# Last stage of a two-layer MoE kernel: fewer clears between gathers, z recomputed instead of stored, the next sequence turned ahead of two whole experts

## The reference, cut to what matters

```
x = x + L0_ffn(L0_cond(x, ...))          # attention, then top-1 of 8 experts
x = x + L1_ffn(L1_cond(x, cond, ...))    # this second line is what the change is about
```

```
gp = leaky(x @ w_gate[e]);  up = x @ w_up[e];  y_e = (gp * up) @ w_down[e]
y  = sum over the token's two experts of topk_w * y_e
z  = y + leaky(x @ sw_gate) * (x @ sw_up) @ sw_down
```

```
pooled = z.mean(axis=1);  logits = pooled @ gate_w.T + gate_b
masked = where(logits < second largest, -inf, logits);  gates = softmax(masked)
out    = sum over e of gates[e] * gelu(z @ expert_w[e].T + expert_b[e])
```

## Time and profile before

| what | us |
|---|---|
| median of 3 runs | 590.78 |
| the runs | 590.07, 590.78, 592.22 |
| span of the profiled execution | 585.8 |
| PE busy | 558.2 (95%) |
| DVE busy | 319.7 (55%) |
| ACT busy | 242.6 (41%) |
| POOL busy | 232.9 (40%) |

### The profile page before, as it was taken

One profiled execution on the slowest core, in us unless ns is written; L12 is line 12 of the kernel. 1 busy time (PEld: TensorE's weight loads), 2 busy tenths in 40 slices (PEclk: granted clock), 3 DMA queues, 4 the chain that ended last, 5 costly groups with the idle time before them and its releaser, 6 DMA issues.

```text
span 585.8 us, 11495 instructions
## 1 busy us (share of the span) xinstructions
PE 558.2 (95%) x3816; PEld 462.9 (79%) x3816; DVE 319.7 (55%) x967; ACT 242.6 (41%) x670; POOL 232.9 (40%) x319
## 2 busy tenths in 40 slices
PE   7999999988999999999999999999999999999895
PEld 4788887744999999988788978888888887776674
DVE  3877757676332225743537754444444444666564
ACT  1555444660211111115544245555555455443342
POOL 2312211042111121007545375555555078777860
PEclk9999999999999999999999999999999999999999
DMA  5960000185995522513396035555555324555562
GB/s 144 390 289 4 1 1 2 63 368 243 333 328 199 184 85 73 155 64 74 72 296 210 0 82 158 157 159 161 161 161 148 99 81 126 170 173 184 158 190 75
DMA packets 51158, 88.16 MB, mean 150 GB/s; under 512 B 9202, under 2 KB 41843, under 8 KB 49556
## 3 DMA queue, kind: packets, MB, share of 16 engines
q1 hardware_dynamic: 42980, 65.16, 31.6%
q0 software_dynamic: 8112, 22.16, 15.7%
HBM read 62.25 MB, written 25.04 MB: 149 GB/s over the span
## 4 chain that ended last, share of the span: by engine, by line
PE 74%; POOL 8%; DVE 7%; issue 4%; DMA 4%; ACT 2%; SPq 1%; POOLq 0%; ACTq 0%; DVEq 0%
PE psum L1326 10%; PE psum L1339 9%; PE psum L1498 9%; PE psum L1586 9%; POOL arena L924 6%; PE psum L1600 5%; PE psum L1182 5%; PE psum L1154 5%; PE psum L1515 4%; PE psum L1578 3%; DMA arena<-x,row_tok 2%; PE psum L1162 2%; PE psum L1661 1%; PE psum L1533 1%; POOL iota_i L954 1%
## 5 line engine op out<-in xcount | busy, mean ns | idle before, releaser
L924 POOL DMA_INDIRECT arena<-x,row_tok x71 | 68.3, 963 | 53.4 <-PE psum L1578 43.4
L924 POOL DMA_INDIRECT arena<-y_sorted,pos_k_i x64 | 64.4, 1006 | 34.7 <-issue 16.2
L1586 PE MATMUL psum<-big_w,arena 128*128 x284 | 73.0, 379 | 0.0
L1916 ACT ACTIVATE arena<-psum,arena 128x128 f32<-128x128 f32 x64 | 18.3, 368 | 106.4 <-PE psum L1326 84.7
L1661 PE MATMUL psum<-big_w,arena 128*128 x248 | 61.3, 379 | 0.0
L1326 PEld LDWEIGHTS psum<-arena,big_w 128*128 128x128 f32 x512 | 59.5, 192 | 1.7 <-issue 1.0
L1326 PE MATMUL psum<-arena,big_w 128*128 128x128 f32 x512 | 59.8, 275 | 0.8 <-DVE arena L2613 0.8
L1498 PE MATMUL psum<-arena,big_w 128*128 128x256 f32 x256 | 59.8, 381 | 0.2 <-ACT arena L1935 0.2
L1586 PEld LDWEIGHTS psum<-big_w,arena 128*128 128x128 f32 x284 | 53.7, 190 | 7.3
L1339 PE MATMUL psum<-arena 128*128 128x256 f32 (+1 forms) x256 | 57.7, 379 | 0.0
L2849 DVE SCALAR_TENSOR_TENSOR arena<-arena 128x128 f32<-128x128 f32 x71 | 20.8, 293 | 60.4 <-ACT arena L2002 57.2
(11 more groups left out here) (338 smaller groups left out, 996.3 us busy)
## 6 DMA issues: line engine op xcount, KB each, us to landing
y_sorted<-arena SPq DMA_DIRECT2D x71, 128.0 KB
big_w<-w SPq DMA_DIRECT2D x8, 1024.0 KB, 5.2
tokens<-x SPq DMA_DIRECT2D x4, 1024.0 KB, 13.2
x<-tokens SPq DMA_DIRECT2D x16, 256.0 KB, 2.6
z_kept<-arena SPq DMA_DIRECT2D x16, 256.0 KB
out<-arena SPq DMA_DIRECT2D x15, 256.0 KB
y_late<-arena SPq DMA_DIRECT2D x16, 128.0 KB, 1.7
big_w<-expert_w_t SPq DMA_DIRECT2D x1, 2048.0 KB, 8.0
```

Of the source, the lines that this page charges most:

```text
L924: pool.indirect_dma_start(dst, None, rows, bass.IndirectOffsetOnAxis(ap=idx, axis=0)).then_inc(done, 16)
L1586: mm = pe.matmul(bank[2 + i % RT][:, 0:2 * M1], c_gt[i % RT][:, k, :], mgu_s[:, k, bass.ds(e, 1), :].rearrange("p a m -> p (a m)"), start= ...
```

## The change

- POOL calls `space()` only after the gathers of the first three sequences (b < RT).
- SP no longer stores `z_t`, and ACT no longer waits for that. In the case of ties POOL gathers the rows of each sequence again (`rows_again`, with the indices copied to `pos_b`), DVE sums them, PE turns and ACT copies them. This adds a branch at the end of POOL's program that waits for `d_all`.
- PE's step c now turns sequence c + 1 first, then loads the indices of c, does the whole first expert of c, the logits of c + 1, and the whole second expert of c.
- DVE's step b now has `sum_choices` of b + 1 ahead of `gates` of b.

```diff
@@ POOL
                 for n, k, done in parts:
                     gather_rows(yk[b % RT][:, 2 * n + k, :], y2_dram, pos_k_i[:, b * NB + n, k:k + 1], done)
-                    space()
+                    if b < RT:
+                        space()
+            with pool.If(more_gates(pool)):
+                with pool.Fori(0, B) as b:
+                    rows_again(b)
@@ SP
-            for b in range(B + 2):
-                if 2 <= b <= B:
-                    sp.wait_ge(d_res, b - 1)
-                    sp.dma_start(outr[:, (b - 2) * NB:(b - 1) * NB, :], res[(b - 2) % RT]).then_inc(d_st[(b - 2) % RT], 16)
-                if b < B:
-                    sp.wait_ge(d_ztc, 2 * b + 2)
-                    sp.dma_start(z_kept[b], z_t[b % RT].rearrange("p k t -> p (k t)")).then_inc(d_keep[b % RT], 16)
+            for b in range(B - 1):
+                sp.wait_ge(d_res, b + 1)
+                sp.dma_start(outr[:, b * NB:(b + 1) * NB, :], res[b % RT]).then_inc(d_st[b % RT], 16)
@@ PE
-            def gated_step(b):
-                front, back, u, v = b < B, b >= 1, b % RT, (b - 1) % RT
-                ahead = b == B - 1
-                if ahead:
-                    gated_bias(b - 1, 1, ids[b - 1][1])
-                    gated(b - 1, v, 1, 0, ids[b - 1][1])
-                if front:
-                    turn_z(b, u)
-                if back:
-                    gated(b - 1, v, 0, 1, ids[b - 1][0])
-                if front:
-                    gate_logits(b)
-                if back and not front:
-                    last_choice(b - 1, v, ids[b - 1][1])
-                elif back and not ahead:
-                    gated_bias(b - 1, 1, ids[b - 1][1])
-                    gated(b - 1, v, 1, 0, ids[b - 1][1])
-                if back and front:
-                    gated(b - 1, v, 1, 1, ids[b - 1][1])
-                if front:
-                    first_expert(b, u)
+            def gated_step(c):
+                u, v = c % RT, (c + 1) % RT
+                more = c + 1 < B
+                if more:
+                    turn_z(c + 1, v)
+                first, second = experts_of(c, u)
+                gated_bias(c, 0, first)
+                gated(c, u, 0, 0, first)
+                gated(c, u, 0, 1, first)
+                if more:
+                    gate_logits(c + 1)
+                    gated_bias(c, 1, second)
+                    gated(c, u, 1, 0, second)
+                    gated(c, u, 1, 1, second)
+                else:
+                    last_choice(c, u, second)
@@ ACT
-            def copy_z(b, u, turn_no):
-                if not isinstance(b, int) or b >= RT:
-                    hold(act, d_keep[u], 16 * turn_no)
+            def copy_z(b, u):
@@ DVE, gated_step
                 if b >= 2:
                     next(outs[b - 2], None)
+                if b + 1 < B:
+                    all_of(sum_choices(b + 1, (b + 1) % RT, (b + 1) // RT))
                 chain = gates(b, b % RT) if b < B else iter(())
                 for _ in range(3):
                     next(chain, None)
-                if 1 <= b:
-                    outs[b - 1] = weigh(b - 1, (b - 1) % RT, (b - 1) // RT)
-                    next(outs[b - 1])
-                if 1 <= b and b + 1 < B:
-                    all_of(sum_choices(b + 1, (b + 1) % RT, (b + 1) // RT))
+                outs[b - 1] = weigh(b - 1, (b - 1) % RT, (b - 1) // RT)
+                next(outs[b - 1])
                 next(chain, None)
```

More of the change, by code:

```diff
@@ L533, in bass_adaln_ffn_kernel @@
         d_ztc = sem("d_ztc")
-        d_keep = [sem(f"d_keep{k}") for k in range(RT)]
         d_back = sem("d_back")
+        d_pos = sem("d_pos")
         d_log = sem("d_log")
@@ L996, in _, with rows_again @@
                 pool.wait_ge(c_st[u], 16 * len(range(u, TILES2, RT)))
+            def rows_again(b):
+                hold(pool, d_e, 2 * B + E2 * b)
+                pool.tensor_copy(pos_b[:, :, :], pos_k_i[:, bass.ds(b * NB, NB), :]).then_inc(d_pos, 1)
+                hold(pool, d_pos, b + 1)
+                for n in range(NB):
+                    for k in range(2):
+                        gather_rows(yk[0][:, 2 * n + k, :], y2_dram, pos_b[:, n, k:k + 1], d_back)
             for b in range(B):
@@ L1631, in _, with turn_all @@
             shared_half(SH_G, 1, 1).then_inc(a_gu, 1)
+            def turn_all(u):
+                for k in range(KD):
+                    for n in range(NB):
+                        mm = pe.transpose(bank[0][:, k * S + n * P:k * S + (n + 1) * P], z_s[u][:, n, k * P:(k + 1) * P], ident[:, :])
+                mm.then_inc(d_zt, 1)
             def turn_z(b, u):
@@ L1637, in turn_z @@
                     pe.wait_ge(d_ztc, 2 * b)
-                for k in range(KD):
-                    for n in range(NB):
-                        mm = pe.transpose(bank[0][:, k * S + n * P:k * S + (n + 1) * P], z_s[u][:, n, k * P:(k + 1) * P], ident[:, :])
-                mm.then_inc(d_zt, 1)
+                turn_all(u)
             def gate_logits(b):
@@ L1724, in _ @@
                 shared_down(s, s % 2)
-            first_expert(0, 0)
-            for b in range(1, B + 1):
-                gated_step(b)
+            for c in range(B):
+                gated_step(c)
             def every_expert(b, first):
-                pe.wait_ge(d_back, 16 * b + 16)
+                hold(pe, d_z, B + b + 1)
+                hold(pe, d_ztc, 2 * B + 2 * b)
+                turn_all(0)
+                hold(pe, d_ztc, 2 * B + 2 * b + 2)
                 for e in range(E2):
@@ L2043, in _ @@
                 shared(s, alone=s == SH_G)
-            copy_z(0, 0, 0)
+            copy_z(0, 0)
             for q in range(NSH):
@@ L2054, in every_expert @@
             def every_expert(b, first):
+                hold(act, d_zt, B + b + 1)
+                act.copy(z_t[0].rearrange("p k t -> p (k t)"), bank[0]).then_inc(d_ztc, 2)
                 for e in range(E2):
@@ L2975, in every_expert @@
             def every_expert(b, first):
+                hold(dve, d_back, 64 * b + 64)
+                for k in range(2):
+                    if k:
+                        hold(dve, d_z1, B + b + 1)
+                    for n in range(NB):
+                        base = z_s[0][:, n, :] if k else p_s[:, bass.ds(b * NB + n, 1), :].rearrange("p a d -> p (a d)")
+                        m = dve.scalar_tensor_tensor(z_s[0][:, n, :], yk[0][:, 2 * n + k, :], w_k[:, k, bass.ds(b * NB + n, 1)], base,
+                                                     ALU.mult, ALU.add)
+                    m.then_inc(d_z if k else d_z1, 1)
                 for e in range(E2):
```

14 lines of the change are left out of this document (3 added, 11 removed).

## The result

The kernel after takes 599.84 us (median of 4 runs, 597.06 to 603.14), the kernel before on the same chip 590.42 us (589.92 to 592.22). The ratio is 1.0152, with a 95% interval of 1.0115 to 1.0188: it is slower by 1.5%, where 581.3 us was forecast and 577 to 587 given as the range. The span of the profiled execution is 597.2 us against 585.8.

The account below looks back on a forecast made before the run. PE's waits bound the last stage's first half, POOL's gathers its end. Last transposes at 560.8, products from 562.2 to 570.4, tail 5.9: span 576.3, plus 5.0 gives 581.3 us, range 577 to 587.

Parts of the forecast that it names:

- The ring of waits: Last stage, PE, DVE and ACT: waits make each step 5.35 us; the new order gives 4.74 to 5.04.
- PE alone with no open load: Bound for the span if only PE's matmuls limit the last stage and index loads are hidden: 572.2 us.
- The index load: PE's register load behind the transposes, last stage: 0.3 us open in each step, bounds 0 and 0.75.
- z not stored: Dropping 16 stores of 256 KB and ACT's waits for them: priced at nothing, at most 0.5 us gained once.
- A gather without its clear: POOL, last stage: 1.25 us straight behind another, 1.365 us taken with the excess; last start 556.4 instead of 566.6.
- a clear costs 0.20 us: POOL, last stage: a gather takes 1.45 us with a clear, 1.25 without, so each clear removed saves 0.20 us.
- as the gathers get denser: Stated sign of being wrong: POOL's excess time per gather has a cause that grows with density; no size given.
- Rival (d): POOL, last stage: packed gathers meet DVE more densely and take 1.73 us each; 599.9 us, chance 0.06.
- Rival (c): POOL, last stage: removing clears wins nothing, gathers still take 1.565 us; 591.5 us, no change, chance 0.07.
- (a): Last stage: small excess on POOL and no open index load on PE; 577.2 to 578 us, chance 0.14.
- (b): Last stage: index load wholly open, 0.75 us a step, or high gather excess; 588.5 us, halfway 585, chance 0.18.

## Why the prediction was wrong, point by point

- **The ring of waits: right.** The order cut it. Undisturbed steps take 4.68 us, just under the 4.74 to 5.04 forecast, and the old order with POOL out of the way still takes 5.35. With plain DMAs the span is 569.3 us, 3 us under the 572.2 worked out for PE alone with no open load.
- **The index load: direction right, size wrong.** 0.3 us a step was put open, with bounds of 0 and 0.75; it is 0. The bias starts 0.44 us behind the transposes (569.43 to 569.87), just their duration. The trace shows why: PE's queue runs ahead of the transposes. The load of this step starts at 568.6 and takes 534 ns, so that it is over before the transposes start at 569.43. The prediction's 0.75 us held only where the load came last. All 16 of these loads in the trace after (duration in ns, least/median/most):

```profile
L1312 PEldq TENSOR_LOAD <-d_top x16: 532/534/542, 492.2 to 587.1; - x16
```

- **z not stored: right**, worth nothing (1.0006).
- **A gather without its clear: the size right, the conclusion wrong.** 1.25 us apart, as the one pair of the earlier trace rows said; the median over the stage is 1.254, the mean 1.32 without POOL's waits for buffers, where 1.365 was taken. By itself this would have let POOL start its last gather at 556. It started it at 572.14, since it waited 18.6 us for DVE, which waited for PE's counts.
- **The step that failed** is the one that priced the clear as a cost of 0.20 us and nothing else: "a clear costs 0.20 us". It also spaced the gathers, and without it PE's counts came up to 8.31 us late, and 14 steps took 24.9 us more than undisturbed ones. Putting the clears back takes the loss away (0.9965 in place of 1.0152). The text saw that a cause on POOL might grow "as the gathers get denser", but looked for it in the gathers' own duration, and took the quiet of one stage at 1.45 us as the behaviour of the machine. The trace of before held the warning, at 265 to 288 us, in the two waits for "remote" shown above.
- **Rival (d)** gave 599.9 us and 599.84 were measured. This is chance: its mechanism, gathers that take 1.73 us, didn't happen. Nor did gathers get longer by meeting DVE more densely: their mean is 1.010 us after and was 1.014 before. In the kernel before, the 21 of 52 gathers behind 486 us that had DVE busy for 90% of their time or more took 1.06 us on the mean, the 20 that had it busy for less than half 0.99; after, 22 took 1.04 and 28 took 0.99.
- **Rival (c)**, nothing won by the clears, is wrong too: with the clears back the kernel is faster than without them, by some 11 us (ratios of 0.9965 and 1.0152), so their removal cost time and wasn't neutral. **Rivals (a) and (b)** had PE's step between them, and (a)'s 577 to 578 us is reached only where no gather is issued, 570 to 575 us.

## What to carry to other kernels

A clear, a wait or any filler between instructions of the same kind may be there for its distance, as the clear of 0.22 us was here (ratio 0.9965 with all of them, 1.0152 without); before it is priced as waste, take it away alone, in one run. Where a list of waits or a chain names "remote" or "an unknown queue" on a single core, compare the end of the instruction that was waited for with the start of the waiter. Here they were 8.3 and 3.1 us apart, and the counts of that work were as late, not the work; its order didn't decide it, since the old order without clears had a count 6.25 us late too, and a ratio of 1.017. In a stage that packs GpSimd's indirect DMAs as these kernels do (counts of PE up to 8.31 us late with gathers 1.25 us apart, up to 3.23 with 1.45, none with two clears), look for late counts of PE, and get the rows by plain DMAs where the addresses allow it (no late count, ratio 0.9707). Whether fewer counts from PE would help, no run here tried.

## What the runs showed of the hardware

- With indirect DMAs of GpSimd 1.25 us apart, semaphore counts of PE came up to 8.31 us late; in the longest cases these come out together 2.0 to 2.3 us after the last of the gathers, in order. At 1.33 us it is up to 8.28, at 1.45 up to 3.23 (the kernel before, at 265 to 289 us), with two clears, 1.70 us or more, none. With plain DMAs of GpSimd none was late, neither 1.22 us apart nor 0.51, though they use the same queue (q0, 2297 packets in 491 to 573 us). All of this is in recorded executions.
- The counts of DVE and ACT that the traces have were on time within 0.02 us (101 and 60 behind 490 us in the kernel after).
- In the kernel after, PE's granted clock fell to 0.50 in or right behind waits of 2.71 to 5.33 us, for 3.4 to 5.6 us of its work: eight products took 3.2 to 3.6 us in place of 1.89. In the longest case that was some 2.7 us on top of the wait. After a wait of 2.19 us (531.48) it didn't fall; with only the last three sequences free it fell at 520.01 after waits of no more than 1.33 us, so the length of the last wait alone doesn't tell.
- An indirect gather of 128 rows keeps POOL 0.95 us busy and lets the next start after 1.25; a plain DMA of the same rows 0.54 and 0.53 us, and one of half the rows hardly less, 0.51 (runs with plain DMAs, whole and halves).
- PE's load of the two indices takes 0.53 us in each of the 16 steps of the kernel after, and was over before the transposes ahead of it started where PE ran full (568.6 to 569.2, and 569.43); in the kernel before it takes 0.54 to 1.08 us, median 0.85.
